# FFN layers of a three-stage kernel: ten uniform jobs become six full jobs and nine mixed tiles

## What is computed

```
h = einsum('bsh,bhk->bsk', x, W_down[role]) + b_down[role]   # 512 -> 256
h = gelu(h)
u = einsum('bsk,bkh->bsh', h, W_up[role]) + b_up[role]       # 256 -> 512
y = x + u
yn = (y - mean) * rsqrt(var + 1e-5)
out = yn * gamma[role] + beta[role]
```

## Time and profile before

| | |
|---|---|
| runs | 2485.14, 2485.66, 2485.71 us, median 2485.66 |
| profiled execution | 2485.6 us, span of the core 2483.9 us |
| PE busy | 2445.9 us, 98% of the span |
| DVE, ACT, POOL busy | 1022.2, 898.6, 402.7 us |
| granted TensorE clock, mean | 0.995 |
| first FFN layer | from about 33 us to about 184 us |
| layers 2 and 3 | from about 2186 us to about 2459 us, then 24 us without PE |

### The profile page before, as it was taken

One profiled execution on the slowest core, in us unless ns is written; L12 is line 12 of the kernel. 1 busy time (PEld: TensorE's weight loads), 2 busy tenths in 40 slices (PEclk: granted clock), 3 DMA queues, 4 the chain that ended last, 5 costly groups with the idle time before them and its releaser, 6 DMA issues.

```text
span 2483.9 us, 27599 instructions
## 1 busy us (share of the span) xinstructions
PE 2445.9 (98%) x11362; PEld 2032.6 (82%) x11362; DVE 1022.2 (41%) x1415; ACT 898.6 (36%) x1227; POOL 402.7 (16%) x312
## 2 busy tenths in 40 slices
PE   8999999999999999999999999999999999999996
PEld 5878888888888888888888888888888888888885
DVE  4774334222333343223243332233433422268776
ACT  4664423222334332223243322232432222346653
POOL 2786000000000000000000000000100000028886
PEclk9999999999999999999999999999999999999998
DMA  7453111211111112111111111102111211144243
GB/s 260 179 206 110 68 51 51 85 51 40 46 68 51 51 51 85 36 49 51 68 52 51 47 72 51 51 32 87 51 35 51 85 51 43 59 162 145 77 145 136
DMA packets 41617, 195.32 MB, mean 79 GB/s; under 512 B 5762, under 2 KB 5762, under 8 KB 24852
## 3 DMA queue, kind: packets, MB, share of 16 engines
q1 hardware_dynamic: 35732, 151.60, 17.8%
q0 software_dynamic: 5760, 41.95, 4.2%
HBM read 162.07 MB, written 31.46 MB: 78 GB/s over the span
## 4 chain that ended last, share of the span: by engine, by line
PE 97%; DVE 1%; DMA 1%; POOL 0%; issue 0%; ACT 0%; DVEq 0%; SPq 0%; ACTq 0%; POOLq 0%
PE pair L57 23%; PE pair L59 23%; PE pair L58 23%; PE pair L963 2%; PE pair L971 2%; PE pair L970 2%; PE pair L962 2%; PE pair L961 2%; PE pair L969 2%; PE pair L454 2%; PE pair L456 2%; PE pair L455 2%; PE pair L420 2%; PE pair L938 1%; PE pair L922 1%; PE pair L452 1%
## 5 line engine op out<-in xcount | busy, mean ns | idle before, releaser
L1336 DVE TENSOR_TENSOR h_lo<-g,h_hi 128x512 fp32r<-128x512 f32 x256 | 178.9, 699 | 745.2 <-ACT h_hi L1160 744.9
L1158 ACT ACTIVATE g<-pair,bias_cols 128x512 f32<-128x512 f32 x256 | 176.6, 690 | 647.8 <-PE pair L59 411.5
L57 PE MATMUL pair<-h_hi,w_hiB 128*128 128x512 f32 x1024 | 399.0, 390 | 0.0
L59 PE MATMUL pair<-h_hi,w_loB 128*128 128x512 f32 x1024 | 398.4, 389 | 0.0
L58 PE MATMUL pair<-h_lo,w_hiB 128*128 128x512 f32 x1024 | 398.4, 389 | 0.0
L57 PE MATMUL pair<-o_hi,w_hiA 128*128 128x512 f32 x768 | 299.2, 390 | 0.0
L59 PE MATMUL pair<-o_hi,w_loA 128*128 128x512 f32 x768 | 298.8, 389 | 0.0
L58 PE MATMUL pair<-o_lo,w_hiA 128*128 128x512 f32 x768 | 298.7, 389 | 0.0
L1113 ACT ACTIVATE w_hiB<-w_raw 128x2048 fp32r<-128x2048 f32 x36 | 69.1, 1920 | 533.8 <-PE pair L59 504.9
L1548 POOL COPY acc<-xr 128x1024 f32<-128x1024 f32 x16 | 15.9, 1036 | 1358.1 <-PE pair L999 1349.8
L59 PEld LDWEIGHTS pair<-h_hi,w_loB 128*128 128x128 f32 x1024 | 192.2, 188 | 40.0
(11 more groups left out here) (236 smaller groups left out, 4371.6 us busy)
## 6 DMA issues: line engine op xcount, KB each, us to landing
w_raw<-in_units_a SPq DMA_DIRECT2D x32, 1024.0 KB
w_raw<-in_units_b SPq DMA_DIRECT2D x32, 1024.0 KB, 4.8
w_raw<-in_units_c SPq DMA_DIRECT2D x16, 1024.0 KB, 4.7
w_raw<-in_w_packed SPq DMA_DIRECT2D x30, 512.0 KB, 4.3
w_raw<-in_rows_packed SPq DMA_DIRECT2D x20, 512.0 KB, 4.6
x<-stage SPq DMA_DIRECT2D x32, 256.0 KB, 2.1
x_tok<-x SPq DMA_DIRECT2D x12, 512.0 KB, 7.5
first_gain<-in_rows_packed SPq DMA_DIRECT2D x10, 512.0 KB, 4.7
```

Source lines behind the costliest of these rows:

```text
L57: pe.matmul(out, lh, rh, start=(i == 0), stop=False)
L59: last = pe.matmul(out, ll, rh, start=False, stop=(i == len(terms) - 1))
L1158: act.activation(g[q % 2][:], bank[q % 4], ACT.Gelu, bias=bias_at).then_inc(gelu_done, 1)
L1336: v.tensor_tensor(h_lo[:, j, cols(n)], g[q % 2][:], h_hi[:, j, cols(n)].bitcast(F32), ALU.subtract).then_inc(hlo_done, 1)
```

## The change

The 64 sequences are now divided in another way. Six full jobs ("octets") hold 48 sequences, 8 of one role each. What is left over of the three roles is put in nine mixed tiles of 128 tokens (two sequences of one role each), three tiles to a job. A layer has nine jobs in the order `KINDS = "OOOMOMOOM"` (O octet with 4 tiles, M mixed with 3 tiles), 33 tiles and not 40. An octet is computed as before. In a mixed job every tile has its own role:

- `pe_mix`: the tokens (xT) are stationary and the weights move. High and low weights of a role stand side by side in `wm` (512 columns), so one matmul with xT_hi gives both products and one of 256 columns with xT_lo adds the third.
- `act_mixed`, `dve_mixed`: ACT copies the left half out of PSUM, DVE adds the right half; the result `pre` has tokens on the partitions, so
- `pe_back`: PE turns it back with two transposes a tile, and gelu, with one instruction a tile and half (the bias differs by tile), reads that.
- The roles of a mixed job take three register loads and not one, on PE, ACT, POOL and (at the end) DVE; POOL and DVE had none before, since gain and shift of all three roles are now loaded once a layer (`sp_load_gain(l)`, 3 DMAs of 512 KB) and picked by register.
- Mixed tiles are gathered and scattered tile by tile, 3 indirect DMAs a job on POOL, not 1.
- The down weights of an octet land in the place of their own low part; the load for octet n waits for the down product of octet n-2. The mixed weights (3 DMAs of 512 KB a layer) are loaded and split once a layer.
- The routing tables take 75 steps on DVE where they took 49; the row numbers of the first gather come at step 47, before at 29.

```diff
+KINDS = "OOOMOMOOM"
+NP = len(KINDS)
+MT = 3
...
-    FIRST_ROWS = 29
+    FIRST_ROWS = 47
...
-    ALL = 49
+    ALL = 75
...
+    def sp_load_mixed(self, sp, l):
+        for r in range(ROLES):
+            sp.dma_start(self.wm[l][:, r, :, BN:2 * BN].bitcast(F32),
+                         self.w_packed[self.layers[l] * ROLES + r, :, 0:self.DOWN].rearrange("p (k n) -> p k n", k=KD))\
+              .then_inc(self.wm_in[l], 16)
...
+    def pe_mix(self, pe, j, roles):
...
+        for t in range(MT):
+            ts = slice(t * P, (t + 1) * P)
+            to = self.turned[t // 2][:, t % 2, :]
+            w = self.wm[l][:, bass.ds(roles[t], 1)]
+            for k in range(KD):
+                pe.matmul(to, self.xT_hi[:, k, ts], w[:, :, k, :].rearrange("p a n -> p (a n)"), start=(k == 0), stop=False)
+                last = pe.matmul(to[:, BN:2 * BN], self.xT_lo[:, k, ts], w[:, :, k, 0:BN].rearrange("p a n -> p (a n)"),
+                                 start=False, stop=(k == KD - 1))
+            last.then_inc(self.mix_mm, 1)
...
+    def pe_job(self, pe, j, roles):
...
+        if self.octet[j]:
+            self.pe_down(pe, j)
+        else:
+            self.pe_mix(pe, j, self.roles_of(pe, j))
+            self.pe_back(pe, j, range(2))
+        if j:
+            self.pe_up(pe, j - 1, range(1), roles)
+        if not self.octet[j]:
+            self.pe_back(pe, j, range(2, MT))
...
             for j in range(2, last.NJ):
-                last.pe_down(pe, j)
-                role = last.role_of(pe, j - 1)
-                last.pe_up(pe, j - 1, range(1), role)
+                roles = last.roles_of(pe, j - 1)
+                last.pe_job(pe, j, roles)
                 if j + 1 < last.NJ:
                     last.pe_transposes(pe, j + 1)
-                last.pe_up(pe, j - 1, range(1, GT), role)
+                last.pe_up(pe, j - 1, range(1, last.T[j - 1]), roles)
```

More of the change, by code:

```diff
@@ L719, in program @@
+        assert o + 2 * half + 4 * six <= places["first_c"] + half
+        folded_at = [sb(f"folded{f}", [P, KD * D], at=where["x_tok"] + half * f) for f in range(2)]
         HIDDEN = HTILES * SB
@@ L807, in _ @@
             sp.wait_ge(routed.dve, routed.ROLE_ROW)
[L808 to L809 removed]
+            for n in range(2):
+                first.sp_load_down(sp, n)
             first.sp_load_bias(sp)
@@ L1031, in _ @@
             fold(range(2))
-            for j in range(NG):
-                first.pe_down(pe, j)
+            roles = None
+            for j in range(NP):
                 if j:
@@ L1174, in _ @@
             act.wait_ge(bias_in, 16)
-            for j in range(NG):
-                role = first.role_of(act, j)
+            for j in range(NP):
+                roles = first.roles_of(act, j)
+                if not first.octet[j]:
+                    first.act_mixed(act, j)
                 if j >= 2:
@@ L1356, in _ @@
                 first.dve_split_up(v, 0, r)
-            for j in range(NG - 1):
-                first.dve_split_down(v, j + 1)
+            for j in range(LAST):
+                if not first.octet[j]:
+                    first.dve_mixed(v, j)
+                first.dve_split_down(v, first.units(j + 1))
                 for m in range(KB):
```

939 lines of the change are left out of this document (567 added, 372 removed).

## The result

The changed kernel takes 2496.3 us (median of 6 runs, 2494.0 to 2497.3), the kernel before 2485.6 us beside it: a ratio of 1.0041, 95% interval 1.0030 to 1.0053. It is slower by 10.7 us. I had forecast 2479. The profiled execution took 2494.1 us by its own time, with a span of 2492.3.

A forecast was written before the change was run, and what follows sets the result against it. PE was taken to bound the FFN loops, with POOL right behind in layer 0. The terms -43.8 + 24.8 + 4 - 1 + 6.6 + 3 = -6.4 against 2485.6 gave 2479 us; own case 2468 to 2490, whole range 2450 to 2508.

The forecast's parts named there:

- Back: mixed loops 5 x 3.0 ..., octets ahead 4 x 1.7 ..., between ..., behind ...: 24.8: Layers 2 and 3: stalls around mixed jobs give back 24.8 us of the 43.8 us of PE work removed.
- the last has no loop behind: Layers 2 and 3: the last mixed job adds no 3.0 us, so only five mixed loops are counted, 15.0 us.
- -13.4: From layer 2's down product of job 2 to the last matmul: -43.8 + 24.8 + 4 + 1.6 for the clock.
- Layer 0 with its start, -1: Start and layer 0: table steps add 3.3 us, POOL holds the crossing into the core stage; -1 us, between -8 and +6.
- the scatter of job 4: End of layer 0: it lands at 167 us, and ACT waits for it before the core stage's first transposes.
- Register loads at 0.75: PE's register loads behind the last up tile are exposed at 0.75 us each, from SP's row; 39 exposed loads.
- Rival A: PE's stream doesn't stop at waits, so register loads are hidden and cost nothing: -35 us, 2450 us; chance 0.25.
- rival B: A register load on PE costs 1.5 us and the clock falls in every mixed loop: 2512 us; chance 0.2.
- Into layer 2, +5.0: Start of layer 2: job 2's down weights queue behind six 512 KB loads, delaying its down product 5.0 us (1 to 9).
- The clock, +4 over five mixed loops: Layers 2 and 3: idle times halve PE's clock, 1.6 us each, in half of five mixed loops: +4 us.
- The tail, +3: Program end: DVE register loads and three last scatters add, one tile less and quicker landing save: +3 us (1 to 5).
- Rival C: POOL late in layer 0 (+6) and job 2's weights late in layer 2 (+5): 2489 us; chance 0.13.

The follow-up runs named there:

- x14: The changed kernel with VectorE's six splits of layer 3's up and mixed weights cut to 2 columns; 2488.5 us.
- x13: The changed kernel with GpSimd multiplying and adding only 4 of 512 elements a token in jobs 6 to 8 of layer 2; 2487.9 us.
- x6: The changed kernel with layer 0's mixed weights issued at 43 us, ahead of job 3's down weights, not at 60.9; 2490.2 us.
- x8: The changed kernel with GpSimd computing 1/sqrt of a job in layer 0 ahead of the gathers of the job four later; 2494.5 us.
- x10: The changed kernel with GpSimd adding beta to only 4 of 512 elements of each token in mixed jobs; 2490.1 us.
- x9: Changed kernel with six edits: residuals first, roles early, job 2 down weights ahead, layer 0 mixed weights early, layer 3 splits late, layer 0 1/sqrt first; 2472.9 us.
- x4: The changed kernel with TensorE reading the three roles of a mixed product twice, 27 loads more; 2514.3 us.
- x5: The changed kernel with layer 2's down weights of job 2 issued right behind the stores, ahead of six loads of mixed weights and gain; 2488.2 us.
- x1: The changed kernel with VectorE's residuals of the job before moved ahead of its splits in mixed loops; 2490.3 us.
- x3: The changed kernel with TensorE reading roles one loop earlier behind the queued product, three loads fewer a mixed job; 2489.1 us.
- x11: x9 with VectorE alone doing gain and shift of the last three jobs, and GpSimd's 1/sqrt ahead of its scatters at the end; 2471.3 us.

## Why the prediction was wrong

The step that failed is the term "Back: mixed loops 5 x 3.0 ..., octets ahead 4 x 1.7 ..., between ..., behind ...: 24.8" of layers 2 and 3. Its loops are right, and they are the sum of steady loops alone. It has no term for the change's own new work outside them: three splits of mixed weights a layer on ScalarE and VectorE, and three up splits moved from three loops of layer 2 into one of layer 3. The diff and the order show both. They cost 8.1 us in three loops, and x14 gives 7.4 of it back with the splits gone, x13 7.2 with GpSimd gone. A smaller one of the same term is "the last has no loop behind": from the last mixed product to the last matmul it took 19.1 us (2443.54 to 2462.65), with 2.39 us of waiting for a residual, 2.6 more than the forecast leaves for it. Against both, the 4 us for the clock were not lost beyond what is in the three loops, and the other loops were 0.6 shorter: 8.1 + 2.6 - 4 - 0.6 = 6.1, so -13.4 became -7.3.

Of some 14.8 us between the forecast and the measured span, 6.1 lie here, 6.1 in layer 0 with its start and the core stage, 2.4 in the tail and 0.3 on the way into layer 2.

**Layer 0 with its start, -1.** It was +5.1 (3.3 + 0.3 + 1.5). The start was right (+3.3 measured), by some luck: 2.9 of it is at the selection matmul (11.01 for 8.07), and in the other runs, which change nothing there, the first down product came anywhere from 36.1 to 37.5. Again a new load was left out: the mixed weights of layer 0, 5.8 us (x6); without it layer 2 begins 0.2 us later than before (2190.7 for 2190.5), where I had 1 earlier. The mechanism that I had for it isn't in the trace: I had the scatter of job 4 hold ScalarE at 167, and ScalarE waits for no scatter there. GpSimd held the loop of job 6 by a 1/sqrt. x8 only moved that wait and x10 took nothing off ahead of it, so how much of layer 0 hangs on GpSimd in the changed kernel stays open; in x9, with the load out of the way, ScalarE waits for GpSimd three times, and nothing was gained. The +1.5 in the core stage is a half clock behind 2.07 us of waiting at its first product; before, the like half clock lay ahead of this mark, in layer 0's stretch.

**Register loads at 0.75.** 0.62 by x4, exposed behind the last up tile as I had it; the estimate from SP's row was 0.13 high, which over 39 loads is 5 us, and the loops came out at forecast since other parts of them were longer: in a mixed loop the loads cost 0.5 us where I had 1.15, the waits on residuals 2.3 where I had 1.8, and the product 0.2 more. That the sum is 15.8 us is partly luck. The 600 ns of the Trainium skill (DMA: Bandwidth & Descriptors, "Latency and other measured facts") was the nearer price here. Rival A (2450; its terms add up to -36, not -35) and rival B (2512, from 0.91 us a load) are both refuted.

**Into layer 2, +5.0.** +5.3, with 1.5 of half clock behind it (forecast 1.6): right, and x5 takes it back.

**The clock, +4 over five mixed loops.** In the changed kernel one of five had it (job 3 of layer 3, 17.2 for 15.8); idle times of 0.6 and 1.1 us did not bring it down. It fell behind idle times of 2.07, 3.10, 3.75, 4.05 and 6.26 us, but not behind one of 2.09 (at 87.9) nor one of 2.39 (at 2454.3), and before it fell behind 0.98 and 1.29: the length of the last wait alone doesn't tell. One more came at the down product of job 2, one in the core stage and two in layer 0. The price differs: at the down product of job 2 of layer 2 it was 1.5 us in the changed kernel and 2.6 to 2.9 in x1, x3, x6, x8, x10 and x13, against 14.5 us for this loop in x5 without it.

**The tail, +3.** +5.4; I had the scatters and the register loads, not what they do to the order of things: the scatters put GpSimd's gain and shift of job 6 later, where they meet VectorE's in full, 3.0 us more. That these 3.0 us are the same contention as in layer 3 is read from the rows; no run takes it away alone.

Rival C's 2489 was nearest by number, and half right: late loads were real, in layer 0 and in layer 2, but the one in layer 2 cost what my own case had, not 5 us more, and layer 0 was late for the load and not for GpSimd's sum. What stays open is the tail: x11 took GpSimd's share away from beside VectorE and gave it to VectorE, which moved the end by about 1 us, and I tried no other order there.

## What to carry to other kernels

A loop by loop estimate of the steady state can be right to 0.4 us and still miss the sum. List every instruction that the change adds or moves outside the loop body (weight splits, loads, reads) and put each into the timeline of its engine, with what the other engines do at that moment. Ahead of an engine's in-order queue ask what stands behind it: here a 6 us split sat ahead of statistics, moments and gelu, and a late load ahead of gelu.

Taking 66 us of work off the busiest engine gave nothing until waits were moved: 12 us with six edits, 20 with two more. In layer 0 the next engine (GpSimd, 60 of 68 us) stood right behind.

## What the hardware showed that I had not expected

A VectorE subtraction of 8 elements (for each partition) took 1.69 us beside GpSimd, until GpSimd's running addition ended; the same of 1024 elements took 1.19 to 1.21 alone and 2.70 beside it. It works the other way too: two additions of GpSimd that met VectorE's splits took 5.75 to 5.78 us, and 4.76 to 4.79 where the splits were cut to a few elements. A register load on TensorE costs 0.62 us when it is exposed, and nothing shows of it where products are queued ahead of it.
